# A Flamingo-style block on one core: the first stage with another order of loads, projections and query readings

## The reference

```
x = x + tanh(g_xattn[0]) * _L0_xattn_ref(_layernorm(x), ctx_1024, ...)   # 16 heads of 16, normed q and k
x = x + tanh(g_ffn[0])   * _L0_ffn_ref(_layernorm(x), ...)               # 32 experts of 96, top 8
x = x + tanh(g_xattn[1]) * _L1_xattn_ref(_layernorm(x), ctx_1024, ...)   # 16 heads of 128, normed q and k
x = x + tanh(g_ffn[1])   * _L1_ffn_ref(_layernorm(x), ...)               # 64 experts of 64, top 4, 2 shared
```

```
y_dca, y_main = y[:, -16:, :], y[:, :-16, :]
q  = _ln((x @ Wq + bq) by heads) ;  k = _ln((y_main @ Wk + bk) by heads) ;  v = y_main @ Wv + bv
kd = _ln((y_dca @ Wkv_dca + bkv_dca) keys by heads) ;  vd = its values
out = (softmax(q k^T / 4) v + softmax(q kd^T / 4) vd) @ Wo + bo
```

## Time and profile before

| | us |
|---|---|
| median of 3 runs | 1856.32 |
| lowest and highest | 1855.57, 1856.35 |
| the profiled execution's own time | 1856.43 |
| its span, first to last instruction | 1854.7 |
| first stage, up to the first score (line 1236) | 51.26 |

### The profile page before, as it was taken

One profiled execution on the slowest core, in us unless ns is written; L12 is line 12 of the kernel. 1 busy time (PEld: TensorE's weight loads), 2 busy tenths in 40 slices (PEclk: granted clock), 3 DMA queues, 4 the chain that ended last, 5 costly groups with the idle time before them and its releaser, 6 DMA issues. The chain is left out here.

```text
span 1854.7 us, 31886 instructions
## 1 busy us (share of the span) xinstructions
PE 1780.7 (96%) x9204; PEld 1303.2 (70%) x9204; DVE 1401.1 (76%) x2298; ACT 1232.0 (66%) x2094; POOL 485.1 (26%) x425
## 2 busy tenths in 40 slices
PE   5899999999999999999999999999999999999998
PEld 3444444468888667786777767777677777888887
DVE  6576666466666889897989989899799996566665
ACT  4576868842332798888988879888898884222232
POOL 4010101215444640005300063000630002544442
PEclk9899999989999999999999999999999999999999
DMA  3523222345433100000000000000000000554452
GB/s 100 112 50 80 66 64 57 73 173 131 112 106 90 54 18 1 0 0 19 18 1 0 0 19 19 0 0 0 1 23 1 8 9 21 116 116 112 106 119 74
DMA packets 109737, 95.90 MB, mean 52 GB/s; under 512 B 72821, under 2 KB 94201, under 8 KB 109017
## 3 DMA queue, kind: packets, MB, share of 16 engines
q1 hardware_dynamic: 109656, 94.88, 20.3%
HBM read 72.94 MB, written 1.44 MB: 40 GB/s over the span
## 5 line engine op out<-in xcount | busy, mean ns | idle before, releaser
L1111 ACT ACTIVATE s_p<-ps,s_g,s_rk 128x256 f32<-128x256 f32 (+1 forms) x832 | 412.6, 560 | 8.8 <-DVE s_dsum L2220 7.8
L1405 PE MATMUL ps<-s_qq,s_ctxT 128*128 (+3 forms) x1248 | 357.3, 399 | 5.9 <-ACT s_p L1111 3.6
L495 PE MATMUL ps<-s_xT,s_wgus 128*128 128x512 f32 x1440 | 348.5, 390 | 0.0
L1405 PE MATMUL ps<-s_ps,s_ctx 128*128 128x512 f32 x1152 | 324.8, 395 | 1.0 <-DVE s_ps L2211 1.0
L495 PEld LDWEIGHTS ps<-s_xT,s_wgus 128*128 128x128 f32 x1440 | 269.9, 188 | 59.4 <-issue 1.5
L972 ACT ACTIVATE s_p<-ps,s_bsm 128x1024 f32<-128x1024 f32 x208 | 222.6, 1114 | 89.9 <-PE ps L1249 57.2
L2211 DVE TENSOR_TENSOR s_ps<-s_p,s_ps 128x512 fp32r<-128x512 f32 x384 | 268.8, 700 | 17.7 <-ACT s_ps L1121 14.2
L1405 PEld LDWEIGHTS ps<-s_qq,s_ctxT 128*128 128x128 f32 (+1 forms) x1248 | 222.8, 184 | 68.4 <-ACT s_p L1111 12.0
L1405 PEld LDWEIGHTS ps<-s_ps,s_ctx 128*128 128x128 f32 x1152 | 215.7, 188 | 56.5 <-DVE s_ps L2211 4.2
L2220 DVE TENSOR_TENSOR s_dsum<-s_dsum,s_p 128x512 f32<-128x512 f32 (+1 forms) x352 | 241.9, 687 | 16.2 <-ACT s_p L1111 12.7
L393 ACT CAST s_hs<-s_hw 128x512 fp32r<-128x512 f32 x120 | 74.5, 621 | 197.9 <-DVE s_hw L1996 197.9
(11 more groups left out here) (282 smaller groups left out, 2358.5 us busy)
## 6 DMA issues: line engine op xcount, KB each, us to landing
s_wB<-w1s SPq DMA_DIRECT2D x64, 256.0 KB, 3.9
s_kT<-s_kst SPq DMA_DIRECT2D x96, 128.0 KB, 2.4
s_kT<-s_kst SPq DMA_DIRECT2D x96, 80.0 KB, 2.1
s_wB<-w0s SPq DMA_DIRECT2D x15, 384.0 KB, 3.5
s_wB<-w0s SPq DMA_DIRECT2D x16, 256.0 KB, 3.7
s_wgu<-in_L_ffn_Wg_dram SPq DMA_DIRECT2D x64, 64.0 KB, 2.8
s_wgu<-in_L_ffn_Wu_dram SPq DMA_DIRECT2D x64, 64.0 KB, 2.6
s_wd<-in_L_ffn_Wd_dram SPq DMA_DIRECT2D x64, 64.0 KB, 2.4
```

Of the source, the lines that this page charges most:

```text
L495: ins = nc.tensor.matmul(ps[:, 4 + g, :], WGUS[f][:, slot, w, g, k, :], XT[f][:, x_, k, n], start=c == 0, stop=c == len(ops) - 1)
L1111: ins = nc.scalar.activation(p1[0:r, SLOT1[t], j, :], ps[0:r, BANK1[t], j * SQ:(j + 1) * SQ], ACT.Exp, bias=g1[0:r, 3:4], scale=rk_col(t, ...
L1405: ins = nc.tensor.matmul(out, lhs(x_), rhs(y_), start=first and n == 0, stop=last and n == 2)
```

## The change

Loads. The first 512 columns of the context of batch 0 (4 tiles, `FIRST0`) are a DMA of their own, issued second. The biases of keys and values and `Wkv_dca` come third and fourth, the tokens fifth, then the two halves of the second bias row, and only then the rest of the context. The biases and `Wkv_dca` have a semaphore of their own, `bkv_loaded`.

TensorE. Ten tiles are projected ahead of the tokens' turning, where it was four. The first waits for the four tiles' own DMA, tile 4 for the rest.

ScalarE. It begins with the values of tiles 0 to 6, and takes the root of the tokens' variance behind them; the copies of the turned tokens stand behind two groups of squares.

VectorE. The centering of `wdca0` and `bkv0` stands ahead of the tokens' statistics. Those are done in two halves behind the readings of tiles 3 and 5, the variance behind tile 6, the norming behind tile 7. Two of the four `take_queries` stand behind `scale_keys`. The third sum of squares stands ahead of the first `take_queries`.

GpSimd fills the half of `vg` for batch 0 first, and no longer waits for all four readings of the queries, but for one.

```diff
@@ sync
-            def load_ctx0(b):
-                sp.dma_start(ctxT0[:, 0:KC], a["ctxT"][b][:, 0:KC]).then_inc(s.ctxT0_loaded, 16)
+            def load_ctx0(b, first=0):
+                sp.dma_start(ctxT0[:, first:KC], a["ctxT"][b][:, first:KC]).then_inc(s.ctxT0_loaded, 16)
...
             sp.dma_start(wkv0[:], a["Wkv0"]).then_inc(s.wkv_loaded, 16)
+            sp.dma_start(ctxT0[:, 0:FIRST0 * P], a["ctxT"][0][:, 0:FIRST0 * P]).then_inc(s.ctx_first, 16)
+            sp.dma_start(bkv0[:, 0, :], a["bkv0"][:, 0, :]).then_inc(s.bkv_loaded, 16)
+            sp.dma_start(wdca0[:], a["Wdca0"]).then_inc(s.bkv_loaded, 16)
             sp.dma_start(x[:], xf).then_inc(s.x_loaded, 16)
+            sp.dma_start(bkv0[0:DROW, 1, :], a["bkv0"][0:DROW, 0, :]).then_inc(s.bkv_loaded, 16)
+            sp.dma_start(bkv0[DROW:P, 1, :], a["bkv0"][DROW:P, 1, :]).then_inc(s.bkv_loaded, 16)
             sp.wait_ge(s.pad_zeroed, 1)
-            load_ctx0(0)
+            load_ctx0(0, FIRST0 * P)
...
@@ gpsimd
-            me.did(g_.memset(vg[:, :, 0:KT - 1, :], 1.0))
...
             for j in range(2):
+                me.did(g_.memset(vg[:, j, 0:KT - 1, :], 1.0))
...
-            pool.sem_inc(s.vg_ones, 1)
-            pool.wait_ge(s.q0_read, 4)
+                pool.sem_inc(s.vg_ones, 1)
+            pool.wait_ge(s.q0_read, 1)
@@ scalar
-            act_std(act, 0)
-            act.wait_ge(s.vg_ones, 1)
-            first_values(range(0, 4))
-            for half in range(2):
-                act_take(act, 0, half, (0, 1))
...
-            for c in range(4):
-                if c < 3:
-                    first_values(range(4 * c + 4, min(4 * c + 8, KT)))
-                square(0, c)
+            act.wait_ge(s.vg_ones, 1)
+            first_values(range(0, 7))
+            act_std(act, 0)
+            first_values(range(7, 9))
+            square(0, 0)
+            first_values(range(9, 10))
+            square(0, 1)
+            for half in range(2):
+                act_take(act, 0, half, (0, 1))
+            first_values(range(10, KT))
+            square(0, 2)
+            square(0, 3)
             key_std(0)
@@ tensor
-                if t == 0:
+                if (b, t) == (0, 0):
+                    pe.wait_ge(s.ctx_first, 16)
+                if t == (0 if b else FIRST0):
                     pe.wait_ge(s.ctxT0_loaded, 48 * (b + 1))
...
-            for t in range(4):
+            for t in range(10):
                 project(0, t)
             pe_turn_start(pe, 0)
-            for t in range(4, KT):
+            for t in range(10, KT):
                 project(0, t)
@@ vector
             center((0,), s.w0_centered)
-            dve.wait_ge(s.x_loaded, 16)
-            statistics(range(NT))
-            normalize(0)
-            dve.wait_ge(s.w0_loaded, 16 * 6)
+            dve.wait_ge(s.bkv_loaded, 16 * 4)
             center((1, 2), s.w1_centered)
...
             for t in range(KT):
                 read_projected(0, t)
+                if t == 3:
+                    dve.wait_ge(s.x_loaded, 16)
+                    statistics(range(0, 4))
+                if t == 5:
+                    statistics(range(4, 8))
+                if t == 6:
+                    variance(range(NT))
                 if t == 7:
+                    apply_std(0, range(NT), 0)
+                if t == 8:
+                    dve.wait_ge(s.w0_loaded, 16 * 2)
                     center((3, 4), s.wq_centered)
+                if t == 9:
                     sum_squares(0, 0)
-                if t == 9:
                     columns()
+                if t == 10:
                     bound_squares()
                 if t == 11:
                     sum_squares(0, 1)
+            sum_squares(0, 2)
             take_queries(0)
-            sum_squares(0, 2)
             sum_squares(0, 3)
             key_variance(0)
-            for j in range(1, 4):
-                take_queries(j)
+            take_queries(1)
             inverse_std(0)
             scale_keys(0, 0)
             scale_keys(0, 1)
+            take_queries(2)
+            take_queries(3)
```

More of the change, by code:

```diff
@@ L81 @@
 QBANK = (4, 7, 5, 6)
+FIRST0 = 4
 E1, F1, TOP1, ND = 64, 64, 4, 4
```

10 lines of the change are left out of this document (4 added, 6 removed).

## The result

The changed kernel takes 1861.59 us (median of 20 runs, 1859.47 to 1864.14), the kernel before 1857.24 (20 runs beside them, 1854.94 to 1860.64). The ratio is 1.0020, 95% interval [1.0014, 1.0026]: 2.6 to 4.8 us slower, about 3.7. The forecast was 1856.5 with a range to 1859.0, and it is outside. Of the 5.1 us between forecast and median, 0.9 is the median of the kernel before, which stood at 1856.32 over three runs and at 1857.24 over twenty. In three of the kernels further down (tokens behind the biases, gap filled, seven products) one of the ten executions took 2918 to 3681 us, and the ratios leave it out.

What follows compares the result with a forecast made beforehand. VectorE's work ahead of `scale_keys` was taken to bound the first stage: 11.2 + 24.3 + 0.75 + 1.2 = 37.45 against 37.25, +0.2 us. Forecast 1856.5 us, own range 1855.6 to 1857.4, wider range 1854.0 to 1859.0.

Steps and rivals of the forecast that it cites:

- work from there: VectorE's work up to `scale_keys`: 25.4 before, less 1.2 for two moved query readings, plus 0.1 for split statistics, 24.3 us.
- tile 7 behind the root: VectorE's reading of tile 7 waits for ScalarE's copy, queued behind the root: a new wait of 0.75 us.
- fourth sum of squares: On VectorE, the fourth sum now directly follows the first query reading and waits 1.2 us for ScalarE's squares.
- the landing of the biases: The last awaited bias DMA lands at 11.2, after 2048 KB at 329 KB/us; VectorE's chain starts 3.0 us late.
- 471 KB/us of the prediction: Fast DMA pace read from 768 KB of context in 1.63 us behind the tokens; throughout, biases would land at 9.4.
- Rival D: Biases land as late as before, at 12.9; `scale_keys` 1.7 us later than in the sum, 1858.2 us; chance 0.10.
- the 2.2 us for values vanish: VectorE's 2.2 us of waiting for ScalarE's value copies goes, as tiles are copied while VectorE waits for the biases.
- rival C: TensorE falls to 1.2 GHz in the gap after tile 9; up to 3.5 us, put at 1858.0 us; chance 0.13.
- the table load: ScalarE's two table loads cost nothing, the second over by 16.7; if behind the root's wait, +1.3 us.
- The start of TensorE: TensorE's first product comes at 6.0 instead of 10.84, but the 4.8 us are spent on VectorE's later start and waits.
- the two moved query readings: Two query readings behind `scale_keys` take 1.2 us off VectorE's work; the 0.75 wait for the last query product goes.
- a shift of `scale_keys` is a shift of the end: Everything behind `scale_keys` keeps its order, so its shift, +0.2 us, passes whole to the first score and the end.

Runs made afterwards that it cites:

- seven products: The kernel before with two query readings behind `scale_keys` and seven overwritten `wkv0` products ahead of the context's landing; ratio 0.9988 to the kernel before.
- experiment 5: The changed kernel with its gap filled: four overwritten products between TensorE's fourth and fifth tile; ratio 0.9999 to the kernel before.
- experiment 11: The changed kernel with one root of one number on ScalarE ahead of its first copy; one run, 1859.27 us.
- Experiment 12: The changed kernel once more, unchanged; one run, 1861.59 us, `scale_keys` at 41.38.
- experiment 2: The changed kernel's engine order and tail with the loads in the order of the kernel before; ratio 1.0007 to the kernel before.
- experiment 6: The changed kernel with tokens loaded last, behind the biases and the rest of the context; ratio 0.9989 to the kernel before.
- experiment 3: The kernel before with two query readings behind `scale_keys` and GpSimd waiting for one reading; ratio 0.9979 to the kernel before.
- experiment 1: The kernel before with the changed order of loads, engines keeping their order; ratio 1.0023 to the kernel before.
- experiment 13: The changed kernel with SyncE issuing the tokens only when the first bias transfer and `wdca0` have landed; one run, 1862.38 us.
- experiment 4: The changed kernel with tokens behind the biases: their DMA issued after both halves of the second bias row; ratio 1.0013 to the kernel before.

## Why the prediction was wrong

Its sum against the profile after, each term from one start to the next:

| term of the sum | predicted | measured |
|---|---|---|
| centering of the biases starts | 11.2 | 13.16 |
| work from there | 24.3 | 24.25 |
| wait at tile 5 | 0 | 1.28 |
| tile 7 behind the root | 0.75 | 0.95 |
| fourth sum of squares | 1.2 | 1.07 |
| `scale_keys` | 37.45 | 40.71 |

The waits are the idle times of VectorE's rows, and the 24.25 is what remains: 40.71 - 13.16 - 3.30. The differences add up to the 3.26 between 37.45 and 40.71. The prediction counted waits as late starts, which are up to 0.1 longer each; counted so, the work is nearer 24.0, an estimate.

**Failed: the landing of the biases, +1.96.** The step was "2048 KB: 6.2 us, so it lands at 5.03 + 6.2 = 11.2", "because the mix of sizes in the sum is the same as there". It was not: the 329 KB/us came from a stretch with 768 KB of context in it, and the changed kernel has 256 KB of context ahead of the biases. Measured are 2048 KB in 13.16 - 4.92, 249 KB/us. Later loads running along explain little of it: all DMA together moved about 2270 KB in that time (282 GB/s for 8.24 us), some 220 KB beyond the sum, against about 100 KB beyond it before. Most of the loss sits between 5 and 8 us, with 222 GB/s on average against 384 before. The 471 KB/us of the prediction is not a pace of the chip either: it put the context behind the tokens, but the two were in flight together, and from 8 to 10 us, when the context's last part came, all DMA moved 427 and 331 GB/s. Landings of 13.0 to 13.8 in the executions of 5, 11 and 12 say that it belongs to the kernel. Rival D (nothing is won, 12.9) was nearest, and its 0.10 was too little for a pace taken from a mean over other transfers.

The law of the Trainium skill ("DMA: Bandwidth & Descriptors", section "Anatomy of one DMA"), by which the forecast gave 9.5 as an estimate, is farther off: 13.16 measured.

**Failed: "the 2.2 us for values vanish", +1.28, and +0.20 at tile 7.** I had looked at tiles 0 to 3, which were ready as said, and for a fall of the clock only behind tile 9 (rival C). But the fifth tile's bank is free only when VectorE has read the first tile, and VectorE stood still until 13.16. The same late landing made a gap of 3.5 us on TensorE, the clock fell in it, and VectorE's readings of tiles 5 and 7 waited for what half-paced products held up. Rival C had the mechanism right and the place wrong. Experiment 5 prices it: 1.84 in all, of which 1.28 is at tile 5 and 0.35 at tile 7. Behind tile 9, where I had looked and had put a price of up to 1.8, the profiled execution shows no fall (the six matmuls took 2.74, the query products 7.07). Experiment 12 shows one there, for a wait of 0.37; in experiments 2 and 6 the turning was slow too (3.61 and 3.35 us), and VectorE's rows hardly show it.

By the Trainium skill ("TensorE: Matmul & The Clock Gate", section "What's actually happening") the slow clock is the default that activity releases; the trace agrees, with 0.50 granted from 16 to 20, and the rule would have pointed here had I listed every gap of the new order.

**Half right: the table load.** "Nothing for both" was true of the first. The second began at 21.73 and not ahead of 16.7, because ScalarE was late with tile 6 by the same low clock, and the root began at its end, at 23.02, half a microsecond behind the variance that it needs. That costs 0.36 (experiment 11), and nothing where the clock stays up or comes back sooner: there the wait at tile 7 is 0.60 with the load in place (experiments 5 and 12). It is the same 0.35 at tile 7 that experiment 5 counts for the clock: either remedy removes it.

**Right.** The start of TensorE (5.90 for 6.0) and that it is worth nothing by itself; the work, within 0.3; the waits at tile 7 and at the fourth sum, within 0.2; the two moved query readings with the product that is no longer waited for, 2.03 in experiment 3 for 1.2 + 0.75; that a shift of `scale_keys` is a shift of the end. On the last: the distance to the first score is 14.0 in every kernel, and the ratio says 3.7 for a shift of 3.46. The prediction wanted the distance from the first score to the end to stay within 0.8 as well, and that asked too much of one execution: it is 1803.4 before, and 1805.6 and 1804.3 in two executions of the changed kernel itself.

**Where the loss sits.** The loads alone cost 4.92 (experiment 1), the order of the engines with its tail 2.04 (experiment 2). Added up that would be 6.96, and it is 3.46: loads and order cost the same wait, and it is paid once. VectorE's first long work starts at 12.30 with the loads alone, at 13.33 with the order alone and at 13.16 with both, against 8.21 before. What remains open is why the DMA moves so little between 5 and 8 us in the new order of loads. It moves 309 GB/s there in experiment 6, where the tokens come last, and experiment 13 shows the slow start of the token transfer; the rest wasn't separated.

## What to carry to other kernels

When a load is moved ahead, price the landing of what is awaited next from packets of its own size in that company, not from a mean over a mix; and then name the transfer that is now last, for it is the next wait (experiments 4 and 6). After each new gap on TensorE ask who frees the bank for the next product, and count the work behind the gap at the low clock. A move of work behind the step that sets the stage's end (experiment 3) needs neither and was the one part that paid; the sum moved ahead of a reading in the same place took more than half of it back, since it had been filling a wait.
